# Turning the softmax shifts into rows: a transpose and four multiplications on VectorE for a product on TensorE

## What is computed

```python
theta = einsum('bchw,kc->bkhw', x, theta_w)            # 32 rows, 1024 pixels
phi   = pool2(einsum('bchw,kc->bkhw', x, phi_w))       # 32 rows, 256 pooled pixels
beta  = softmax(einsum('bnk,bkm->bnm', theta, phi), axis=-1)
g     = pool2(einsum('bchw,kc->bkhw', x, g_w))         # 128 rows, 256 pooled pixels
o_in  = einsum('bcm,bnm->bcn', g, beta)
x1    = gamma * einsum('bchw,kc->bkhw', o_in, o_w) + x
out   = x1 + einsum('fc,bchw->bfhw', tpl, x1)          # tpl: 27 taps, circular, 256x256
```

## Time and profile before

| | us |
|---|---|
| median of 3 runs | 278.06 |
| lowest, highest | 276.76, 278.17 |
| the profiled execution | 277.08 |
| its span on the core | 275.4 |
| TensorE busy | 268.0 (97% of the span) |
| VectorE busy | 239.1 (87%) |
| ScalarE busy | 243.1 (88%) |
| GpSimd busy | 152.2 (55%) |

### The profile page before, as it was taken

The page is one execution under the profiler, slowest core; times in us unless marked ns, Lnnn a source line. Parts: engine busy times, 40 slices in busy tenths (PEclk is TensorE's granted clock), DMA queues, the critical chain, the costliest instruction groups (busy, mean ns, idle before and its releaser), DMA issues.

```text
span 275.4 us, 4412 instructions
## 1 busy us (share of the span) xinstructions
PE 268.0 (97%) x1210; PEld 212.5 (77%) x1210; DVE 239.1 (87%) x402; ACT 243.1 (88%) x532; POOL 152.2 (55%) x78
## 2 busy tenths in 40 slices
PE   7899999999999999999999999999999999999894
PEld 3477778787878878787887878888787888878683
DVE  4999899898989989898998989899898989989843
ACT  3999899998999999898999989999898989988662
POOL 5486646574664657456564755656475466636000
PEclk9999999999999999999999999999999999999999
DMA  7977085582838558183765718466572846235034
GB/s 201 262 201 207 27 231 167 182 212 94 187 126 231 167 169 217 82 198 129 219 179 169 212 60 209 146 211 187 167 171 85 224 148 200 45 152 94 14 141 154
DMA packets 17380, 44.57 MB, mean 162 GB/s; under 512 B 2654, under 2 KB 3578, under 8 KB 16122
## 3 DMA queue, kind: packets, MB, share of 16 engines
q1 hardware_dynamic: 16826, 44.26, 55.8%
q10 hardware_dynamic: 544, 0.20, 0.3%
HBM read 17.45 MB, written 16.78 MB: 124 GB/s over the span
## 4 chain that ended last, share of the span: by engine, by line
PE 91%; ACT 3%; DVE 2%; DMA 2%; issue 0%; SPq 0%
PE psY L968 10%; PE psY L947 7%; PE psY L948 7%; PE psY L949 7%; PE psV L1086 5%; PE psY L1086 5%; PE psY L1070 5%; PE psV L1070 5%; PE psV L947 3%; PE psX L1024 3%; PE psV L948 3%; PE psV L949 3%; PE psV L1091 3%; PE psX L1008 3%; PE psY L1054 3%; PE psV L1054 3%
## 5 line engine op out<-in xcount | busy, mean ns | idle before, releaser
L446 POOL TENSOR_TENSOR prob_lo<-prob,prob_hi 128x1024 fp32r<-128x1024 f32 x30 | 72.3, 2411 | 63.4 <-ACT prob L525 36.2
L439 POOL TENSOR_TENSOR x_lo<-x_raw,x_hi 128x1024 fp32r<-128x1024 f32 x30 | 72.0, 2401 | 34.3 <-ACT x_hi L492 32.0
L492 ACT CAST x_hi<-x_raw 128x1024 fp32r<-128x1024 f32 x30 | 31.5, 1050 | 4.7 <-PE psY L1054 4.4
L514 ACT ACTIVATE psX<-psX,neg_max 128x256 f32<-128x256 f32 x60 | 26.8, 446 | 3.1 <-DVE neg_max L752 2.5
L514 ACT ACTIVATE psZ<-psZ,neg_max 128x256 f32<-128x256 f32 x60 | 27.4, 470 | 0.0
L690 DVE TENSOR_TENSOR thetaphi<-psY,thetaphi_rest 64x512 f32<-64x512 f32 x30 | 20.5, 682 | 2.0
L947 PE MATMUL psY<-x_hi,g_hi_w 128*128 128x512 f32 x56 | 22.2, 396 | 0.0
L948 PE MATMUL psY<-x_lo,g_hi_w 128*128 128x512 f32 x56 | 22.2, 396 | 0.0
L949 PE MATMUL psY<-x_hi,g_lo_w 128*128 128x512 f32 x56 | 22.1, 396 | 0.0
L696 DVE TENSOR_TENSOR theta_aug<-thetaphi,theta_aug 32x512 fp32r<-32x512 f32 x30 | 20.5, 683 | 0.9
L683 DVE TENSOR_REDUCE phi_pool<-thetaphi 32x128 f32<-32x512 f32 x30 | 20.2, 675 | 1.0
(11 more groups left out here) (185 smaller groups left out, 761.3 us busy)
## 6 DMA issues: line engine op xcount, KB each, us to landing
x_raw<-x SPq DMA_DIRECT2D x30, 512.0 KB, 5.0
out<-y SPq DMA_DIRECT2D x15, 1024.0 KB, 4.0
x_edge<-x_hi SPq DMA_DIRECT2D x64, 104.0 KB
x_edge<-x_lo SPq DMA_DIRECT2D x32, 104.0 KB
x_raw<-x SPq DMA_DIRECT2D x4, 256.0 KB, 4.7
out<-y SPq DMA_DIRECT2D x4, 256.0 KB, 2.5
band_rev<-ring SPq DMA_DIRECT2D x2, 128.0 KB, 7.0
proj_raw<-proj_wT ACTq DMA_DIRECT2D x1, 128.0 KB, 4.8
```

Of the source, the lines that this page charges most:

```text
L439: nc.gpsimd.tensor_tensor(x_lo[:, par, :, cols], x_raw[:, par, :, cols], x_hi[:, par, :, cols].bitcast(F32), ALU.subtract).then_inc(x_lo_r ...
L446: nc.gpsimd.tensor_tensor(prob_lo[:, h], prob[:, h], prob_hi[:, h].bitcast(F32), ALU.subtract).then_inc(prob_lo_ready, 1)
L492: nc.scalar.copy(x_hi[:, par, :, cols], x_raw[:, par, :, cols]).then_inc(x_hi_ready[h], 1)
L514: last = nc.scalar.activation(tiles[:, t, :], tiles[:, t, :], ACT.Exp, bias=neg_max[:, col:col + 1], accum_out=exp_sum[:, col:col + 1])
```

## The change

The product with the identity and its PSUM rows go. shift_parts gets 32 columns (the 16 further ones stay zero), and VectorE turns it in one instruction, which transposes each square of 32x32 by itself: for pixels 32q to 32q+31 of every tile the 16 values stand afterwards at partitions 32q to 32q+15, in 32 columns of PSUM (shift_turned_ps). Four multiplications, one for each q, spread a square over the tiles of theta_aug's rows, masked with own_tile. own_tile has one number per tile now and lies at the four start partitions, filled by GpSimd. One call covers both halves of an image; the first image keeps its two halves, with 4 tiles each. ident is no longer rounded; the transposes of g wait for ident itself. shift_rows stands ahead of the copy out_of_psum, and in the first image ahead of sum_thetaphi and pool_phi.

```diff
-        own_tile = sb("own_tile", [SHIFT_ROWS, 2 * NT, P])
+        own_tile = sb("own_tile", [P, 2 * NT])
...
-        shift_parts = sb("shift_parts", [P, 2 * NT, 2], F32R)
+        shift_parts = sb("shift_parts", [P, SQUARE // 2, 2], F32R)
...
-            def shift_rows(i, par, h):
-
-                dve.wait_ge(shift_rows_done, from_second(1, i, par, 1))
-                row = shift_ps[:, :].rearrange("q (o n) -> q o n", o=1).broadcast_to([SHIFT_ROWS, NT, P])
-                rows = theta_aug[R_SHIFT:K_AUG, par, :].rearrange("q (t n) -> q t n", n=P)
-                tiles = slice(h * NT, (h + 1) * NT)
-                nc.vector.tensor_tensor(rows[:, tiles, :], row, own_tile[:, tiles, :],
-                                        ALU.mult).then_inc(shift_rows_ready, 1)
+            def turn_shifts(turned):
+
+                return nc.vector.transpose(turned, shift_parts[:, :, :].rearrange("p t s -> p (t s)").bitcast(F32))
+
+            def spread_shifts(turned, par, first, end):
+
+                rows = theta_aug[R_SHIFT:K_AUG, par, :].rearrange("r (t n) -> r t n", n=P)
+                for q in range(0, P, SQUARE):
+                    row = turned[q:q + SHIFT_ROWS, :].rearrange("r (o n) -> r o n", o=1).broadcast_to([SHIFT_ROWS, end - first, SQUARE])
+                    own = own_tile[q:q + SHIFT_ROWS, first:end].rearrange("r (t o) -> r t o", o=1).broadcast_to([SHIFT_ROWS, end - first, SQUARE])
+                    last = nc.vector.tensor_tensor(rows[:, first:end, q:q + SQUARE], row, own, ALU.mult)
+                return last
+
+            def shift_rows(i, par):
+
+                dve.wait_ge(shift_parts_ready, from_second(1, i, par, 1))
+                turn_shifts(shift_turned_ps).then_inc(shift_turned_ready, 1)
+                dve.wait_ge(shift_turned_ready, from_second(1, i, par, 1))
+                spread_shifts(shift_turned_ps, par, 0, 2 * NT).then_inc(shift_rows_ready, 2)
...
             def shift_rows0(h):
 
+                dve.wait_ge(shift0_parts_ready, h + 1)
+                turn_shifts(first_shift_turned_ps[h]).then_inc(shift0_turned, 1)
                 if h == 0:
-                    dve.wait_ge(own_tile_ready, 3)
-                dve.wait_ge(shift0_rows_done, h + 1)
...
+                    dve.wait_ge(own_tile_ready, 6)
+                dve.wait_ge(shift0_turned, h + 1)
+                spread_shifts(first_shift_turned_ps[h], 0, h * NT, (h + 1) * NT).then_inc(shift_rows_ready, 1)
...
-            round_ident()
...
             shifts0(0)
+            shift_rows0(0)
             sum_thetaphi(0, 1, 0)
-            shift_rows0(0)
             pool_g(0, 1, 0)
             shifts0(1)
             w2_high()
+            shift_rows0(1)
             pool_phi(0, 1, 0)
-            shift_rows0(1)
...
                 shifts(ni, npar)
+                shift_rows(ni, npar)
                 out_of_psum(i, par, 0, 0)
-                for h in range(2):
-                    shift_rows(ni, npar, h)
...
-            def shifts_to_rows(i, par):
-
-                pe.wait_ge(shift_parts_ready, from_second(1, i, par, 1))
-                nc.tensor.matmul(shift_ps, shift_parts[:, :, :].rearrange("p t s -> p (t s)"), ident_r[:],
-                                 start=True, stop=True).then_inc(shift_rows_done, 1)
...
-                shifts_to_rows(ni, npar)
```

More of the change, by code:

```diff
@@ L50, in attention_then_channel_filter @@
     K_AUG = R_SHIFT + SHIFT_ROWS
+    SQUARE = 32
+    TURNED = SQUARE
     REACH = 13
@@ L121, in attention_then_channel_filter @@
         w2_ps = turn_ps[1][:, 0:C]
-        shift_ps = psZ[0:SHIFT_ROWS, 0, 0:P]
+        shift_turned_ps = psZ[:, 1, 4 * NT:4 * NT + TURNED]
         ln_sum_ps = psZ[:, 1, 0:2 * NT]
         shift_sum_ps = psZ[:, 1, 2 * NT:4 * NT]
-        first_shift_ps = [ps[0:SHIFT_ROWS, 0, 0:P] for ps in scores_ps]
+        first_shift_turned_ps = [ps[:, 1, 4 * NT:4 * NT + TURNED] for ps in scores_ps]
         first_ln_sum_ps = [ps[:, 1, 0:NT] for ps in scores_ps]
@@ L169, in attention_then_channel_filter @@
         shift0_parts_ready = sem("shift0_parts_ready")
-        shift0_rows_done = sem("shift0_rows_done")
+        shift0_turned = sem("shift0_turned")
         x_loaded = [[sem(f"x_loaded{h}{par}") for par in range(2)] for h in range(2)]
@@ L198, in attention_then_channel_filter @@
         shift_parts_ready = sem("shift_parts_ready")
-        shift_rows_done = sem("shift_rows_done")
+        shift_turned_ready = sem("shift_turned_ready")
         shift_rows_ready = sem("shift_rows_ready")
@@ L390, in own_tiles @@
             def own_tiles():
-                nc.gpsimd.memset(own_tile[:], 1.0).then_inc(own_tile_ready, 1)
+                first = own_tile[0:SHIFT_ROWS]
+                nc.gpsimd.memset(first, 1.0).then_inc(own_tile_ready, 1)
                 pool.wait_ge(own_tile_ready, 1)
-                nc.gpsimd.affine_select(out=own_tile[:], in_=own_tile[:], compare_op=ALU.is_ge, fill=0.0, base=0,
-                                        pattern=[[-2, 2 * NT], [0, P]], channel_multiplier=1).then_inc(own_tile_ready, 1)
+                nc.gpsimd.affine_select(out=first, in_=first, compare_op=ALU.is_ge, fill=0.0, base=0,
+                                        pattern=[[-2, 2 * NT]], channel_multiplier=1).then_inc(own_tile_ready, 1)
                 pool.wait_ge(own_tile_ready, 2)
-                nc.gpsimd.affine_select(out=own_tile[:], in_=own_tile[:], compare_op=ALU.is_ge, fill=0.0, base=1,
-                                        pattern=[[2, 2 * NT], [0, P]], channel_multiplier=-1).then_inc(own_tile_ready, 1)
+                nc.gpsimd.affine_select(out=first, in_=first, compare_op=ALU.is_ge, fill=0.0, base=1,
+                                        pattern=[[2, 2 * NT]], channel_multiplier=-1).then_inc(own_tile_ready, 1)
+                for q in range(SQUARE, P, SQUARE):
+                    pool.wait_ge(own_tile_ready, 2 + q // SQUARE)
+                    nc.gpsimd.tensor_copy(own_tile[q:q + SHIFT_ROWS], first).then_inc(own_tile_ready, 1)
+                pool.wait_ge(own_tile_ready, 6)
             def x0_low(h, t):
@@ L670, in _ @@
             nc.vector.memset(shift_parts[:].bitcast(F32), 0.0).then_inc(shift_parts_zeroed, 1)
-            def round_ident():
-                dve.wait_ge(ident_ready, 1)
-                nc.vector.tensor_copy(ident_r[:], ident[:]).then_inc(ident_r_ready, 1)
             def tp_weights_low():
@@ L827, in shifts0 @@
                     dve.wait_ge(shift_parts_zeroed, 1)
-                else:
-                    dve.wait_ge(shift0_rows_done, 1)
                 nc.vector.tensor_copy(shift_parts[:, tiles, 0], first_shift_sum_ps[h]).then_inc(shift0_hi_ready, 1)
@@ L900, in _ @@
             shifts(0, 1)
-            shift_rows(0, 1, 0)
+            shift_rows(0, 1)
             out_of_psum(0, 0, 1, 0)
-            shift_rows(0, 1, 1)
             def image(i, par):
@@ L987, in g_transposed @@
                 if is_first(i, par):
-                    pe.wait_ge(ident_r_ready, 1)
+                    pe.wait_ge(ident_ready, 1)
                 elif not is_second(i, par):
@@ L1139, in fold_weights @@
                 last.then_inc(w2_done, 1)
[L1141 to L1145, removed]
             pe.wait_ge(idle_operand_ready, 1)
```

9 lines of the change are left out of this document (2 added, 7 removed).

## The result

| | before | changed |
|---|---|---|
| median of 20 runs, us | 276.75 | 278.00 |
| lowest, highest | 276.53, 278.46 | 277.67, 279.87 |
| the profiled execution, its span | 277.08, 275.4 | 277.82, 276.1 |

The changed kernel takes 1.0044 of the time before, with a 95% interval of 1.0028 to 1.0059: 1.2 us slower. Single executions of one kernel lie up to 2.2 us apart (277.67 to 279.87). So stretches are compared from a fixed instruction on.

The account below looks back on a forecast made before the run. TensorE was taken as the bound, within hundredths of waiting for VectorE. First image +1.3, second +0.8, steady images -0.5, last +0.1 gave +1.7 us on a mean of 277.5: 279.2, with an 8-in-10 range of 277.0 to 282.3.

Parts of the forecast that it names:

- rival C: Start-up loss mostly hidden because ScalarE's chain carries the first image: 0.5 for 1.3, 0.4 for 0.8; +0.5, 278.0; chance 0.12.
- VectorE's first image costs 1.3: First image: VectorE has no pause, rows cost 1.47 a half, +1.5 us at L712; L1008 moves by 1.3.
- the cover that I allowed: First image: L1008 put down to ScalarE's L525, so VectorE had up to 0.23 us to spare.
- The second image costs 0.8, by y behind the rows: Second image: g projection waits for y, now behind the rows, and starts at 35.08 instead of 34.29: +0.8 us.
- The path to L1024: 0.03 + 0.20 + 0.03 + 1.77: Steady image, VectorE from parts to rows: transpose 0.20, four multiplications 1.77 with gaps of 0.03; 2.03 in all.
- Rival A: The four multiplications overlap at spacing 0.34, so TensorE gets its whole 0.10 an image: -0.4, 277.1; chance 0.20.
- the rule cited: VectorE holds an instruction until earlier ones finish if its input or output starts in another 32-partition group in that memory.
- That is 0.04 better than now: Steady image: L1024 starts at 147.16 instead of 147.20, not 0.10 earlier; 13 x 0.04 = -0.5 us.
- TensorE's saving turns into a wait: Steady images: of TensorE's 0.10 saving only 0.04 arrives, as TensorE waits for VectorE's rows in every image.
- Without both, L1024 could start at 147.10: Steady boundary: without L1015 (0.06) and the slower pair behind it (0.04), L1024 could start 0.10 earlier.
- The last image, +0.1: Last image: with y and gT_lo behind the rows, L947 starts at 261.65 where it was 261.58: +0.1 us.
- Rival B: VectorE becomes the bound: transpose 0.28, multiplications 0.45, path 2.23; +4.9, 282.4; chance 0.20.

Follow-up runs that it names:

- two products: Changed kernel with TensorE's shift product and the old order brought back for the first two images; median 276.22 us, ratio 0.9982 to the kernel before.
- the one-square kernel: Changed kernel, all four multiplications reading the square at partition 0 and subtracting a mask of 1000; median 275.78 us, ratio 0.9954 to the kernel before.
- without the product: Kernel before without TensorE's shift product from the second image on, VectorE's passes subtracting a mask of 1000; median 276.48 us, ratio 0.9982.
- the order alone: Kernel before with the two row multiplications ahead of the copy to y inside the loop, product kept; median 276.51 us, ratio 0.9990.

## Why the prediction was wrong

The direction was right and the causes of the loss were those named, but 279.2 was forecast and 278.00 measured. Two terms of the sum were mis-sized. The base was 0.8 too high: I took the mean of four executions, 277.52, two of them near 278.1, where only five of the 20 runs of that kernel lie; their median is 276.75. And of the +1.7 us of change, +1.2 was measured, because the steady images gave back twice what I had put down. That rival C's total is 278.0 is chance: its hidden start did not come.

- **VectorE's first image costs 1.3.** Right: 1.34, and 1.50 at L712, for 0.2 of which ScalarE had the cover that I allowed. The product back in that image returned 1.3.
- **The second image costs 0.8, by y behind the rows.** Right in size: 2.13 - 1.34 = 0.79, and gone with two products in the old order.
- **The path to L1024: 0.03 + 0.20 + 0.03 + 1.77.** Nearly: the transpose took 0.23 for 0.20, the four 1.73 for 1.77. Rival A's overlap does not happen, and the one-square kernel shows why. One inference beside it was wrong: own_tile's start partition in SBUF changes together with the PSUM input's, so by the rule cited each of the four is held even if PSUM inputs did not count, and rival A did not hang on them.
- **"That is 0.04 better than now": the failed step.** Mis-sized by half. An image gained 0.08, so the 13 steady ones brought -1.04 and not -0.5. L1024 moved by 0.06 (2.71 to 2.65), and TensorE's stretch from L1024 to the scores shrank from 7.54 to 7.52 in the mean. I had shifted L1024 in one image and left the rest of the round as it was, with differences of hundredths taken thirteen times; a round added up from its four stretches would have shown how little 0.04 could be trusted. What shortens the 7.54 stays open: the six products of the g projection take 1.40 before and 1.38 after. It is neither the missing product nor the order, since they take 1.40 both without the product and in the order alone.
- **TensorE's saving turns into a wait.** Right, and stronger than I said: without the product and nothing else an image gains 0.01. "Without both, L1024 could start at 147.10" missed that the 0.17 between the transposes and L1024 held a wait already; TensorE's own limit is 0.14. What I missed besides is that the gain of the steady part comes with the order. Rows ahead of y give 16.12 with the product in place. The transpose adds 0.01 an image on that and saves 0.3 in the last image, and with its places in the first two images it costs 2.1 there.
- **The last image, +0.1.** Shift instruction to L947: 3.82 for 3.77. Right.
- **Rival B** (over 16.25) and **C** (L1008 before 26.5 us) did not come.

## What to carry to other kernels

An engine that is busy without a pause need not be the bound: add up the round from one wait to the same wait an image later, and see which stretch each engine owns, before crediting a saved instruction. Where the trace draws a product longer than its distance to the next, a short wait is hidden in the bar: compare distances of starts between kernels. Moving a small product from the full engine to another pays only if that engine has free time just there; at the start, where VectorE had none, it cost twice what the steady images brought. When a change moves work and reorders it, time the reordering by itself.

## What the runs showed of the hardware

Four operations of 16x256 float32 whose inputs start at partitions 0, 32, 64 and 96 start 0.43 us apart; four from one start partition 0.33. A transpose of 128x32 float32 from SBUF to PSUM takes 0.23, and two of them without a wait 0.32 together. A product of 16 columns of weights with 128 columns holds TensorE for 0.06 and costs 0.04 more at the pair behind it: from the last L1091 to the transposes it is 1.26 us with it and 1.17 without. A wait of 0.13 us between two products leaves TensorE busy for 100% of an image by the trace.
